# A four-layer network on one core: in the first layer, the state sum goes from TensorE to GpSimd, the expert sum to VectorE, and the B and C rows come from TensorE instead of a DMA

## What is computed

```
    def step(h, inp):
        x_t, dt_t, B_t, C_t = inp
        dA = jnp.exp(dt_t[:, :, None] * A[None, :, :])
        dB = dt_t[:, :, None] * B_t[:, None, :]
        h = dA * h + dB * x_t[:, :, None]
        y = jnp.einsum('bds,bs->bd', h, C_t) + D * x_t
        return (h, y)
    ...
    xc = lax.conv_general_dilated(...) + conv_b[None, :, None]      # 4 taps, one channel each
    x_conv = jax.nn.silu(jnp.swapaxes(xc, 1, 2))
    dt = jax.nn.softplus(x_conv @ dt_w.T + dt_b)
    Bm = x_conv @ B_w.T + B_b
    Cm = x_conv @ C_w.T + C_b
    y = _selective_scan(x_conv, dt, A, Bm, Cm, D)
    y = y * jax.nn.silu(z)
    return y @ out_w.T + out_b
```

```
    h = jax.nn.gelu(jnp.einsum('btd,edf->ebtf', x, w1) + b1[:, None, None, :], approximate=False)
    y = jnp.einsum('ebtf,efd->ebtd', h, w2) + b2[:, None, None, :]
    output = jnp.einsum('ebtd,bte->btd', y, comb)
```

## Time and profile before

| | us |
|---|---|
| three runs: lowest, median, highest | 2132.44, 2134.67, 2136.69 |
| the profiled execution: its time | 2140.97 |
| its span, first to last instruction | 2139.2 |
| first layer in it: first state begins | 54.75 |
| first layer in it: gating of the last sequence (L1979) begins | 593.40 |

### The profile page before, as it was taken

One profiled execution on the slowest core, in us unless ns is written; L12 is line 12 of the kernel. 1 busy time (PEld: TensorE's weight loads), 2 busy tenths in 40 slices (PEclk: granted clock), 3 DMA queues, 4 the chain that ended last, 5 costly groups with the idle time before them and its releaser, 6 DMA issues.

```text
span 2139.2 us, 24172 instructions
## 1 busy us (share of the span) xinstructions
PE 1667.5 (78%) x8792; PEld 813.2 (38%) x8792; DVE 1137.4 (53%) x2368; ACT 1015.3 (47%) x1654; POOL 66.9 (3%) x88
## 2 busy tenths in 40 slices
PE   5888889888969879788886766767677577776876
PEld 2454445445534445444443222322222322222442
DVE  3665586468575574664753323324321777574522
ACT  4566565575503224032235767566676023333575
POOL 1000000000000000000000000000000000000003
PEclk8999999999979999999997767667576567887898
DMA  4312232125131002010032311203011022021002
GB/s 161 94 52 58 59 70 60 48 72 163 36 94 46 16 2 60 1 46 15 2 104 107 98 31 30 74 15 102 17 41 34 26 76 57 29 57 53 1 2 64
DMA packets 91621, 116.31 MB, mean 54 GB/s; under 512 B 10096, under 2 KB 71536, under 8 KB 91120
## 3 DMA queue, kind: packets, MB, share of 16 engines
q1 hardware_dynamic: 89808, 110.05, 17.9%
q0 software_dynamic: 1696, 4.72, 0.8%
HBM read 83.27 MB, written 31.46 MB: 54 GB/s over the span
## 4 chain that ended last, share of the span: by engine, by line
PE 39%; DVE 18%; ACT 10%; issue 3%; SPq 1%; DMA 1%; POOL 0%; DVEq 0%; POOLq 0%; ACTq 0%
PE ps L1158 8%; PE ps L862 5%; DVE neg_max L1903 5%; PE ps L861 4%; PE ps L873 4%; ACT scratch L1500 3%; ACT ps L1482 2%; PE ps L1071 2%; PE ps L1022 2%; DVE hidden L1679 2%; DVE gated L1675 2%; ACT tanh L1388 1%; ACT weights_even L1500 1%; DVE mixture_sum L1701 1%; PE ps L1126 1%
## 5 line engine op out<-in xcount | busy, mean ns | idle before, releaser
L1500 ACT ACTIVATE scratch<-ps 128x1024 f32<-128x1024 f32 x272 | 274.3, 1020 | 230.6 <-PE ps L1128 62.7
L1903 DVE TENSOR_REDUCE neg_max<-ps 128x2 f32<-128x1024 f32 (+2 forms) x224 | 232.2, 1067 | 101.9 <-PE ps L1071 101.0
L884 PE MATMUL ps<-xnt,weights_even 128*128 128x512 f32 x256 | 143.9, 691 | 77.9 <-ACT hidden L1371 43.4
L1158 PE MATMUL ps<-scratch,values 128*32 128x512 f32 (+3 forms) x1280 | 186.7, 669 | 11.3 <-DVE heads_out L1923 5.7
L1388 ACT ACTIVATE tanh<-ps 128x512 f32<-128x512 f32 x88 | 52.5, 597 | 286.1 <-PE ps L862 286.1
L1482 ACT ACTIVATE ps<-ps 128x512 f32<-128x512 f32 x256 | 150.8, 589 | 60.6 <-PE ps L1117 60.6
L1765 DVE TENSOR_TENSOR_SCAN scratch<-scratch 128x512 f32<-128x512 f32 x128 | 149.0, 1204 | 1.1 <-ACT scratch L1453 1.1
L1675 DVE SCALAR_TENSOR_TENSOR gated<-tanh,ps 128x512 f32<-128x512 f32 x88 | 60.3, 686 | 156.6 <-ACT tanh L1388 156.5
L1916 DVE COPY head_out<-ps 128x512 f32<-128x512 f32 x48 | 33.0, 687 | 188.8 <-PE ps L1158 188.5
L924 PE MATMUL ps<-scratch,consts 128*128 128x512 f32 x256 | 121.9, 608 | 4.9 <-DVE scratch L1771 4.9
L861 PE MATMUL ps<-xnt,weights_odd 128*128 128x512 f32 x176 | 108.1, 699 | 12.8 <-DVE hidden L1679 8.7
(11 more groups left out here) (308 smaller groups left out, 2736.0 us busy)
## 6 DMA issues: line engine op xcount, KB each, us to landing
scratch<-state_rows SPq DMA_DIRECT2D x64, 512.0 KB, 4.8
scratch<-parts_scratch SPq DMA_DIRECT2D x288, 96.0 KB, 2.3
parts_scratch<-weights_even SPq DMA_DIRECT2D x168, 128.0 KB, 2.4
weights_odd<-in_l SPq DMA_DIRECT2D x8, 519.5 KB, 6.4
weights_even<-in_l SPq DMA_DIRECT2D x1, 4096.0 KB, 15.4
weights_odd<-in_l SPq DMA_DIRECT2D x1, 4096.0 KB, 14.9
parts_scratch<-gated SPq DMA_DIRECT2D x15, 128.0 KB, 2.4
slots_scratch<-head_out SPq DMA_DIRECT2D x5, 256.0 KB, 5.2
```

The lines of the kernel that those rows point to most:

```text
L884: pe.matmul(ps[:, up_bank(0, n), :], W(0, "w1")[:, P * f:P * (f + 1)], tokens(n // NF[0]), start=True, stop=True).then_inc(q[0, "up_ready" ...
L1158: mm = pe.matmul(ps[32 * i:32 * i + 32, PV, q0:q0 + n], lhs, buf[:, slot, col:col + n], start=first_, stop=True, skip_group_check=True)
L1500: act.activation(dst, src, ACT.Exp).then_inc(q[l, "exp_done"], 1)
L1903: ins = dve.tensor_reduce(dst, ps[:, base:base + 2, col:col + n], AX.X, ALU.max, negate=True)
```

## The change

- The B and C rows no longer pass through DRAM. Their projection is split into three bfloat16 parts (steps `b1`, `b2`, `b3`; `bcs`), and for every state TensorE spreads its B row and its C row over the 128 partitions by one bfloat16 matmul each with a selector of ones (`state_rows`, a new constant `sel` of 1 MB), into PSUM banks 0/1 or 2/3 in turn. VectorE's two kinds of products read these banks.
- The state sum is made by GpSimd: `y += product`, two adds of 128x512 per state, with y opened by ScalarE as D times x_conv (`y0`). `hc` has two buffers instead of three.
- The scaling of the expert's down product by ScalarE and its adding by TensorE are gone; VectorE does both in four instructions (`expert_mixed`), at the expert step, that is between an even state and the odd one after it.
- Heads of later sequences share bank MI with tails and weight turning; they are spread over steps 0 to 14.
- The weights of the second layer come by two DMAs instead of nine; the memsets of `values` stand earlier.

```diff
-HEAD0_AT = {0: (("hx", 0),), 1: (("hx", 1),), 2: (("hx", 2),), 3: (("hx", 3),), 4: (("cv", 0), ("hz", 0)), 5: (("cv", 1),),
...
+HEAD0_AT = {0: (("hx", 0),), 2: (("hx", 1),), 3: (("hx", 2),), 4: (("hx", 3),), 5: (("hz", 0),), 6: (("cv", 0), ("zs", 0)),
...
-            for name in ("dt", "dtx", "zs"):
+            for name in ("dt", "dtx", "zs", "y"):
...
-            return (2, UP)[f % 2] if l == 0 else UP
+            return (UP, PV)[f % 2] if l == 0 else UP
...
-            return (0, 1, 2, 3, 0, 1, 3, 0, 1)[k] if b == 0 else 3
+            return (0, 1, 2, 3, 0, 1, 2, 3, 0)[k] if b == 0 else MI
...
-            def added(n):
-                for g in range(2):
-                    pe.wait_ge(q[0, "hc_ready"], 2 * n + g + 1)
-                    mm = pe.matmul(ps[:, g, :], eye, hc[n % 3][:, g, :], start=False, stop=True, skip_group_check=True)
-                mm.then_inc(q[0, "state_added"], 1)
+            def state_rows(n):
+                pe.wait_ge(q[0, "bcs_ready"], n // NST + 1)
+                if n >= 2:
+                    pe.wait_ge(q[0, "hc_ready"], 2 * (n - 1))
+                for k in range(2):
+                    mm = pe.matmul(ps[:, 2 * (n % 2) + k, :], sel[0:6 * NST, n % NST + NST * k, :],
+                                   bcs[n // NST % 2][0:6 * NST, :], start=True, stop=True)
+                mm.then_inc(q[0, "bc_rows"], 1)
...
                     elif what == "s":
-                        if n:
...
-                            added(n - 1)
+                        if n == 0:
+                            pe.wait_ge(s_sel, 16)
+                            pe.wait_ge(q[0, "head_seen"], HEAD0_USES)
+                            state_rows(0)
+                        if n + 1 < STATES:
+                            state_rows(n + 1)
...
+            def expert_mixed(m):
+                b, e = m // E0, m % E0
+                cw, facc = cws[b % 2], faccs[b % 2]
+                dve.wait_ge(q[0, "y_ready"], 4 * m + 5)
...
+                for j in range(TB):
+                    ins = stt(facc[:, j, :], ps[:, YB, P * j:P * (j + 1)], cw[:, j, e:e + 1], facc[:, j, :],
+                              ALU.mult, ALU.add)
+                ins.then_inc(q[0, "y_free"], 1)
...
-                    tt(ub[:, g, :], sets[b % 2]["dtx"][:, g, :], bc_rows[n % RING][:, 0, :], ALU.mult).then_inc(q[0, "u_ready"], 1)
+                    tt(ub[:, g, :], sets[b % 2]["dtx"][:, g, :], ps[:, 2 * (n % 2), :], ALU.mult).then_inc(q[0, "u_ready"], 1)
...
-                    elif what in ("f", "mb1") and l == 0:
-                        pass
+                    elif what == "mb1":
+                        mixture_begin(l, b)
+                    elif what == "f" and l == 0:
+                        if n:
+                            expert_mixed(n - 1)
...
+                if what == "s":
+                    y = sets[b % 2]["y"]
+                    if n % NST == 0:
+                        pool.wait_ge(q[0, "y_begun"], 2 * (b + 1))
+                    for g in range(2):
+                        if n % NST:
+                            pool.wait_ge(q[0, "state_added"], 2 * n + g - 1)
+                        pool.wait_ge(q[0, "hc_ready"], 2 * n + g + 1)
+                        pool.tensor_tensor(y[:, g, :], y[:, g, :], hc[n % 2][:, g, :], ALU.add)\
+                            .then_inc(q[0, "state_added"], 1)
```

More of the change, by code:

```diff
@@ L175, in constants @@
     slope = 0.5 ** np.arange(NH)
+    sel = np.zeros((P, 2 * NST, P), f)
+    for n in range(2 * NST):
+        sel[[n, 2 * NST + n, 4 * NST + n], n] = 1
     c16 = blob([
@@ L411, in first_layer @@
     out = [(what, 0, 0, n) for what, n in HEAD0_FIRST]
[L412 removed]
+    out += [("da", 0, 0, 0), ("f", 0, 0, 0)]
     for b in range(NB):
@@ L416, in first_layer @@
             out.append(("s", 0, b, n))
+            if n == 0:
+                out += [("cw", 0, 0, 0), ("mb0", 0, 0, 0), ("mb1", 0, 0, 0)]
             if s % 2 == 0 and n + 2 < STATES:
@@ L433, in first_layer @@
                 out.append(("fl", 0, b, 0))
[L434 to L442, removed]
-    out += [("ac", 0, b, EXPERTS - 1)] + follow[1:2] + [("tg", 0, b, 0), ("yg", 0, b, 0), ("op", 0, b, 0)] + follow[2:3] + [("cb", 0, b, 0)] + follow[3:4]
+            if s == 15:
+                out.append(("tg", 0, b, 0))
+            if b == NB - 1 and s >= 14:
+                out.append(follow[s - 14])
+    out += [("yg", 0, b, 0), ("op", 0, b, 0)] + follow[2:3] + [("cb", 0, b, 0)] + follow[3:4]
     out += [("nm", 0, b, 0), ("tr", 0, b, 0)]
@@ L696, in program @@
         s_w = [sem(f"weights_in{l}") for l in range(4)]
-        rows_in = [sem("state_rows_in%d" % n) for n in range(RING)]
+        s_sel = sem("selectors_in")
         s_experts = sem("experts_in0")
-        all_in = {1: 16 * 9, 2: 48, 3: 32}
+        all_in = {1: 32, 2: 48, 3: 32}
         s_out = sem("out_written")
@@ L954, in weights_turned @@
                 mm.then_inc(q[l, "cwt_turned"], 1)
-            def expert_added(m):
-                pe.wait_ge(q[0, "y_free"], m + 2)
-                pe.matmul(ps[:, PV, :], eye, qk[:, m % 2, :], start=False, stop=True, skip_group_check=True)\
-                  .then_inc(q[0, "expert_added"], 1)
             def biases_mixed(l, b):
@@ L1740, in constants0 @@
                 for n in range(2 * KC):
-                    own.add(ts(diag[:, n, :], eye, small[:, n:n + 1], None, ALU.mult))
-                for g in range(2):
-                    ins = ts(diag[:, 2 * KC + g, :], eye, W(l, "d")[:, g:g + 1], None, ALU.mult)
+                    ins = ts(diag[:, n, :], eye, small[:, n:n + 1], None, ALU.mult)
                 ins.then_inc(q[l, "diagonals_ready"], 1)
@@ L2231, in rows @@
                     sp.dma_start(slope, blobs["slope"]).then_inc(q[l, "rows_ready"], 16)
-            sp.wait_ge(q[3, "zeros_ready"], 1)
-            for b in range(NB):
-                states(b)
-            sp.wait_ge(q[0, "hc_ready"], 2 * STATES)
+            zero_slots()
+            next_weights()
+            sp.wait_ge(q[0, "state_added"], 2 * STATES)
             rows(1)
```

190 lines of the change are left out of this document (86 added, 104 removed).

## The result

The changed kernel takes 2209.43 us (median of 4 runs, 2202.67 to 2212.53), the kernel before 2135.68 in the same comparison (4 runs, 2132.44 to 2140.55). The ratio is 1.0336, with a 95% interval from 1.0310 to 1.0363. The forecast was 2159, with a range up to 2184: slower was right, and two thirds of the size were missing. The profiled execution has a span of 2209.9 us, 70.7 more than before.

The account below looks back on a forecast made before the run. TensorE bounded the layer before; afterwards TensorE and VectorE take turns. Start, 15.6 us pairs, head extras and end put the last gating at 617.9 instead of 593.40: 2134.67 + 24.5 = 2159 us, range 2118 to 2184.

Parts of the forecast that it names:

- VectorE's own extras: VectorE's head work (gates, `ds` 2.4, `cb` 3.7, b1, b3): hidden in the 5.2 us it waits in each block.
- Turns of TensorE and VectorE: In each pair of states, TensorE's block, the mixing and one state follow in series; TensorE idles 5.4 us.
- Clean pair, 15.6 us: Two states without head work: TensorE's block 9.8 us, mixing 1.1, one state 4.64; 12.65 us before.
- Half clock 1.9 us: About 4.3 us at half speed at the head of each TensorE block after its gap, losing 1.9 us.
- Start: First sequence: dt ready about 49.4 us, state 0 begins about 58.5, pair 0 ends at 85.2.
- Extras of head work, 15.8 us per full sequence: Next head's work at even steps, lengthening TensorE's block above 9.8 us: 15.8 us on top of eight pairs.
- The end, 18.4 us: Layer's last pair, from rows and downs (6.3 us) through state 63 to the last add: 18.4 us, ending at 617.9.
- Nothing behind the layer: After the last gating no time was added: its 24.5 us delay went unchanged into the kernel's time.
- GpSimd: GpSimd's state-sum adds: 1.2 us each, at most 2.85, hidden, with no wait for them on VectorE.
- half speed lasts longer: Rival: TensorE stays at 1.2 GHz for 6 us per block, about 30 pairs lose 0.8 us more, 2183 us; chance 0.11.

Follow-up runs that it names:

- two reorderings that break the turn: Changed kernel with VectorE's mixing behind the odd state, 2124.67 us; or with TensorE's down products ahead of the hidden chunks, 2071.06 us.
- the filled kernel: Changed kernel with five more matmuls that nobody reads, behind TensorE's rows in its gap while VectorE does the odd state; 2236.14 us.
- short adds: Changed kernel with GpSimd adding only 4 of each product's 512 columns, so the first layer's output is not the reference's; 2196.78 us.
- gate weights at 10: Changed kernel with only the next head's gate weights on VectorE moved from behind state 11 to behind state 10; 2201.29 us.

## Why the prediction was right, and where it was wrong

The direction and the mechanism of a clean pair were right; the size was not: 2209 us measured, 2159 forecast, 2184 the upper end of the range. The step that failed is a term of the sum, the extra cost of head work, and in it the sentence that VectorE's own extras, `ds` among them, cost nothing.

- **Turns of TensorE and VectorE**: right. The wait before the mixing (4.8 us here, 150 in total) and TensorE's gap (5.49; the forecast had 5.4) are there, and either of two reorderings that break the turn removes VectorE's wait in a clean pair and shortens TensorE's gap, to at most 2.9 us.
- **Clean pair, 15.6 us**: measured 15.9, mean of the last sequence's seven steps 110.97 / 7; those seven took 1.8 us more than the 109.2 forecast. Half clock 1.9 us: measured 2.2. Without it the forecast had 13.7, and the filled kernel took 13.71 to 13.72.
- **Start**: dt was forecast for 49.4 and ready at 49.6, state 0 was forecast for 58.5 and began at 58.55; pair 0 ended at 87.3 instead of 85.2.
- **Extras of head work, 15.8 us per full sequence**: this is the term that failed. Measured 23.4 (150.2 less 8 x 15.85). From odd scan to odd scan the steps 0 to 14 take 17.0, 16.5, 17.0, 21.4, 17.9, 18.3, 19.9 and 22.2 us; the forecast had 16.7, 16.7, 16.7, 20.7, 16.7, 18.2, 19.3 and 15.6. Seven of the eight are within 1.2 us of it. The eighth, step 14, is 6.6 off, three times, 19.8 us. The forecast said of VectorE's own extras, `ds` among them, that they "lie in the 5.2 us that it waits in each block". But `ds` stands at step 13, with the bias copy 4.1 us behind an odd state, and ScalarE's Exp at step 14 waits for it, with the Gelus queued behind. Moving that Exp gave 5.7 to 6.3 us per step back. So of the 7.6 us by which the extras were too small, 6.3 (22.2 less 15.85) are this one wait. For the gate weights the sentence was right in effect, as their own run showed.
- **The end, 18.4 us**: 20.8, from 631.86 to the gating at 652.66. Rows and down products took 7.3 us at half clock instead of 6.3, and the last query parts 3.9 instead of 2.3, because they stand beside GpSimd's add (below).
- **Nothing behind the layer**: the last gating came 59.3 us later, the end of the span 70.7. Of the 11.4 us between, 2.5 are the out projection and what follows it at half clock, after 12.13 us of idling:
```profile
654.02 3.75 PE L931 MATMUL ps<-weights_even,scratch 128*128 128x128 f32 x16 [12.13 <-DVE scratch L1971]
```
The same took 2.02 us before. Of the other 9, 6.3 stand in one stretch of the last layer. First the kernel before, then the changed one, same code and the same number of matmuls:
```profile
1933.40:2024.00 90.60, 64.57 (x478) 26.67 (x482) 40.79 (x62) 36.90 (x45) 5.18 (x5) 0.81 0.11 32
...
1998.70:2095.60 96.90, 72.94 (x478) 28.10 (x482) 41.04 (x62) 36.91 (x45) 5.19 (x5) 0.72 0.11 30
```
The granted clock is 0.72 there instead of 0.81; why is not known. It need not be the change: from the last state's scan to the end, 15 kernels, nearly alike in that part, took between 1540.9 us (short adds, granted clock 0.81) and 1564.6 us (changed, 0.79; before, 1552.4 at 0.80), and single runs of the kernel before range from 2130.28 us at a granted clock of 0.848 to 2156.20 at 0.833.
- **GpSimd**: an add at 1.2 us, measured 1.25; no wait for it, right. That it slows VectorE's scans (and the products of dt, which took 1.37 and 2.17 us at step 14 instead of 1.21 and 1.22 with short adds) was not foreseen. In sum it cost the layer nothing in this order: with short adds step 14 gained 1.5 us, and step 12 lost 1.2.
- **Sum**: 2.1 (start) + 19.8 (step 14) + 8.7 (the other steps of three sequences) + 1.8 (last sequence) + 2.4 (end) = 34.8 us in the layer, and 11.4 behind it; some 5.8 of the 8.7 are the clean pair's 0.25 us, 23 times. That makes 46.2 of the 50.4 us missed. The other 4 are no work of the kernel: the forecast took the profiled execution to be 6.3 us longer than the median, as before, and it was 2.3 longer. The rival "half speed lasts longer" came out nearer (2183) but for a reason that wasn't its own: the clean pair grew by 0.3 us, not 0.8. The time lay outside the range, because the bounds were drawn around the clock and not around the extras.

## What to carry to other kernels

When an engine's result is needed between two steps of another engine's chain, look at what the first has queued ahead of it: the order inside the block (here, down products before chunks) decided between 3% slower and 3% faster, with the same instructions. For every piece of work that is called hidden, name the step at which it stands and who waits for it next, on every engine; an Exp that waits at the head of ScalarE's queue holds up the Gelus that another engine waits for. Here a recurring gap of 5.5 us cost its own length and then 2.2 us of half clock behind it; with gaps of 1.20 us the clock stayed at full, and with gaps of at most 2.9 us in most clean pairs.

## What the runs showed of the hardware

- While a GpSimd add runs, VectorE's scans and other operations with two operands in SBUF take longer, casts too, and those with one operand in PSUM do not: the two scans beside an add take 3.12 us instead of 2.33, an operation on 32 columns 0.94 and 1.30 instead of 0.18, a cast 1.17 instead of 0.43, and the products with rows in PSUM stay at 1.25 to 1.28. The Trainium skill ("SBUF — State Buffer", section "Who interferes with whom") has this rule, by the port that the two share; the traces agree. Here are the gate weights beside an add, in the kernel with them at step 10:
```profile
316.82 2.49 POOL L2123 TENSOR_TENSOR scratch<-scratch 128x512 f32<-128x512 f32 x2 [2.92 <-DVE scratch L1763]
317.19 0.94 DVE L1637 TENSOR_TENSOR combine<-consts,top_index_f 128x32 f32<-128x32 f32 x1
318.06 1.30 DVE L1638 TENSOR_TENSOR combine_second<-consts,top_index_f 128x32 f32<-128x32 f32 x1
319.28 0.16 DVE L1639 TENSOR_SCALAR gate_small<-gate_small 128x4 f32<-128x4 f32 x1
```
- Half clock can take back what a step gains. With the gate weights at 10, step 12 is 1.2 us longer than in the changed kernel: the Gelus come no later, TensorE has waited 2.68 us for them instead of 0.45, and then two chunks take 2.96 us instead of 2.45 and the first 16 instructions of the down products 2.68 instead of 1.95. Three kernels (changed, short adds, gate weights at 10) have full sequences of 150.17 to 150.19 us, although their steps differ by up to 1.6 us. That the sums agree so closely is not explained.
